# The recurrence's input copied out of PSUM by ScalarE before the scan, and V's bias folded into the output bias, in a transformer block fused with a mixture of experts

## The reference

```python
xn = _layernorm(x)
h = _layernorm(xn, ln1_g, ln1_b)
q, k, v = heads(h @ WQ + bQ), heads(h @ WK + bK), heads(h @ WV + bV)   # 16 heads of 8
scores = where(0 <= i - j < 128, q @ k.T / sqrt(8), -inf)
ao = softmax(scores) @ v
attn_out = ao @ WO + bO
u = h @ Bw                                    # 64 states
s_t = A * s_{t-1} + u_t                       # a scan over the 512 tokens
g = sigmoid(h @ Wg + bg)
x1 = xn + g * attn_out + (1 - g) * (s @ Cw)
s = x1 + gelu(_layernorm(x1, ln2_g, ln2_b) @ W1 + b1) @ W2 + b2
out = x + s * silu(mixture of 8 experts, top 2, of xn)
```

## Time and profile before

| | us |
|---|---|
| median of 3 runs (915.14 to 916.11) | 915.94 |
| the profiled execution, as timed | 917.65 |
| the same, its span in the trace | 915.9 |
| TensorE busy | 841.9 (92%) |
| VectorE busy | 712.3 (78%) |
| ScalarE busy | 721.0 (79%) |
| GpSimd busy | 484.2 (53%) |

### The profile page before, as it was taken

The page is one execution under the profiler, slowest core; times in us unless marked ns, Lnnn a source line. Parts: engine busy times, 40 slices in busy tenths (PEclk is TensorE's granted clock), DMA queues, the critical chain, the costliest instruction groups (busy, mean ns, idle before and its releaser), DMA issues.

```text
span 915.9 us, 37757 instructions
## 1 busy us (share of the span) xinstructions
PE 841.9 (92%) x15768; PEld 547.1 (60%) x15768; DVE 712.3 (78%) x1785; ACT 721.0 (79%) x1251; POOL 484.2 (53%) x786
## 2 busy tenths in 40 slices
PE   4569999999999999999999999999999999998996
PEld 2335666657566665756666575666657566665645
DVE  7666868879787887978788797878879787786635
ACT  4337888888788888888788888888888888877785
POOL 6417446382735638283653827366382736445352
PEclk9758999999999999999999999999999999999999
DMA  5952417133351613334261323416133341610101
GB/s 127 227 88 84 75 43 142 56 104 44 119 80 56 142 55 103 44 125 75 66 130 56 104 43 123 76 61 136 55 100 47 113 76 50 135 44 7 31 2 36
DMA packets 85597, 75.14 MB, mean 82 GB/s; under 512 B 9457, under 2 KB 79154, under 8 KB 85426
## 3 DMA queue, kind: packets, MB, share of 16 engines
q1 hardware_dynamic: 83346, 71.93, 34.9%
q10 hardware_dynamic: 2080, 0.79, 0.4%
HBM read 36.26 MB, written 30.15 MB: 73 GB/s over the span
## 4 chain that ended last, share of the span: by engine, by line
PE 64%; DVE 14%; issue 10%; ACT 7%; POOL 2%; DMA 2%; SPq 1%; POOLq 0%; DVEq 0%; ACTq 0%
PE ps L571 11%; PE ps L513 8%; PE ps L843 6%; PE ps L805 6%; PE ps L502 5%; PE ps L794 3%; PE ps L590 2%; DVE mx L1221 2%; PE ps L528 2%; PE ps L811 2%; PE ps L585 2%; ACT h L1077 2%; PE ps L719 2%; PE ps L781 2%; DVE act_t L1368 2%
## 5 line engine op out<-in xcount | busy, mean ns | idle before, releaser
L1221 DVE TENSOR_REDUCE mx<-ps 128x2 f32<-128x320 f32 (+1 forms) x512 | 219.7, 466 | 101.9 <-PE ps L528 100.8
L1004 ACT ACTIVATE pt<-ps 128x1024 f32<-128x1024 f32 (+1 forms) x256 | 232.9, 914 | 39.5 <-PE ps L502 37.2
L1487 POOL TENSOR_SCALAR_AFFINE_SELECT pt<-pt 128x512 f32<-128x512 f32 x256 | 162.3, 637 | 140.5 <-ACT pt L1004 139.5
L513 PE MATMUL ps<-kd,qz 48*32 48x160 bf16 (+1 forms) x4096 | 146.1, 236 | 13.8 <-issue 6.7
L502 PE MATMUL ps<-qz,kd 51*32 51x256 bf16 (+1 forms) x4096 | 153.6, 261 | 0.8 <-issue 0.7
L794 PEld LDWEIGHTS ps<-m,act_t 128*128 128x128 f32 x1024 | 128.1, 191 | 39.6 <-DVE act_t L1368 23.6
L571 PE MATMUL ps<-pt,va 128*32 128x256 f32 (+1 forms) x2048 | 145.2, 364 | 2.1 <-POOL pt L1490 0.9
L794 PE MATMUL ps<-m,act_t 128*128 128x128 f32 x1024 | 140.0, 280 | 7.6 <-DVE act_t L1368 5.7
L513 PEld LDWEIGHTS ps<-kd,qz 48*32 48x32 bf16 x4096 | 77.9, 92 | 105.9 <-issue 52.3
L1490 POOL TENSOR_SCALAR_AFFINE_SELECT pt<-pt 128x512 f32<-128x512 f32 x192 | 122.1, 636 | 0.0
L1037 ACT ACTIVATE lin<-ps,mbias 128x512 f32<-128x512 f32 x128 | 87.5, 684 | 35.5 <-DVE act_t L1368 22.9
(11 more groups left out here) (187 smaller groups left out, 1560.1 us busy)
## 6 DMA issues: line engine op xcount, KB each, us to landing
qz<-qk_parts SPq DMA_DIRECT2D x32, 384.0 KB, 6.4
kd<-qk_parts SPq DMA_DIRECT2D x32, 384.0 KB, 10.0
qk_parts<-qp SPq DMA_DIRECT2D x16, 384.0 KB, 3.1
qk_parts<-kp SPq DMA_DIRECT2D x16, 384.0 KB, 2.8
xl<-L_attn_x SPq DMA_DIRECT2D x16, 256.0 KB, 3.5
qk_parts<-qp SPq DMA_DIRECT2D x16, 256.0 KB, 3.1
qk_parts<-kp SPq DMA_DIRECT2D x16, 256.0 KB, 2.9
xnr<-xn SPq DMA_DIRECT2D x16, 256.0 KB, 2.5
```

The lines of the kernel that those rows point to most:

```text
L513: nc.tensor.matmul(ps[QG * c:QG * (c + 1), 4 + par, w * pr:w * (pr + 1)], qz[q][rows, 2 * g + pr, P * i + QG * c:P * i + QG * (c + 1)], kd ...
L1004: nc.scalar.activation(to, src, ACT.Exp, scale=SCALE).then_inc(exp_ok.sem, 1)
L1221: nc.vector.tensor_reduce(mx[:, i, HG * g + pr:HG * (g + 1):2], src, AX.X, ALU.max).then_inc(mx_ok.sem, 1)
L1487: sel1 = nc.gpsimd.affine_select(out=pt[:, s, :, 0:P], in_=pt[:, s, :, 0:P], compare_op=ALU.is_ge, fill=0.0, base=0, pattern=[[0, HG], [1, ...
```

## The change

Two things are changed.

**The scan's input.** From batch 2 on, ScalarE copies `u` (64 x 512 f32) from bank 7 into `h0` in SBUF (`u_out`, behind the exponential of chunk 8); `h0` is free there, since its rows were turned at chunk 3. `project_v` now waits for this copy (`u_in`) and no more for the scan. The scan reads `h0` and stands one chunk later in VectorE's order, behind the maxima of chunk 10 where it stood behind those of chunk 9. The last part of `route_mix` moves one chunk later too (`MIX`).

**V's bias.** `project_v` drops its bias matmul. At the start, one matmul of `bvc` (zero but for column 64, which is `bV`) with `WO` gives `bV @ WO` in row 64 of a bank, and `bias_out` adds it to the row of `ncw` that holds `bO`. What prepared `bV`'s bf16 parts is gone; the broadcast load of `bV` becomes a load of one column among the later weights.

```diff
-MIX = (9, 9, 13, 21)
+MIX = (9, 9, 13, 23)
...
             def project_v(m):
                 k = bank_of(m, "v")
-                pe.wait_ge(*(done(st_ok, m) if m >= 2 else done(v_ok, m - 1)))
+                pe.wait_ge(*(done(u_in, m - 2) if m >= 2 else done(v_ok, m - 1)))
...
-                add_bias(k, 0)
-                for t in range(NT):
-                    mm = nc.tensor.matmul(bank_t(k)[:, t], turned(m)[:, P * t:P * (t + 1)], wv[:], start=False, stop=True, skip_group_check=True)
+                for t in range(NT):
+                    mm = nc.tensor.matmul(bank_t(k)[:, t], turned(m)[:, P * t:P * (t + 1)], wv[:], start=True, stop=True)
...
                         logits(0)
+                        pe.wait_ge(*done(gth_ok, 1))
+                        nc.tensor.matmul(bank(7)[:, 0:P], bvc[:], wo[:], start=True, stop=True).then_inc(bvo_ps.sem, 1)
...
+            def u_out(m):
+                act.wait_ge(*done(u_ps, m))
+                act.wait_ge(*done(hT_ps, m))
+                act.wait_ge(*done(st_ok, m - 1))
+                nc.scalar.activation(h0[0:N].rearrange("p t d -> p (t d)"), bank(bank_of(m, "u"))[0:N], ACT.Copy).then_inc(u_in.sem, 1)
...
+                        if n == AT_U:
+                            u_out(b + 2)
...
-                for dst, src in ((wv, ob[:, 0]), (rows["bV"], ob[:, 1])):
-                    nc.vector.tensor_copy(dst[:].rearrange("p (s c k v) -> p s c k v", s=NS, c=HG, k=2), paired(src)).then_inc(values_set.sem, 1)
+                nc.vector.tensor_copy(wv[:].rearrange("p (s c k v) -> p s c k v", s=NS, c=HG, k=2), paired(ob[:, 0])).then_inc(values_set.sem, 1)
...
+            def bias_out():
+                dve.wait_ge(bvo_ps.sem, 1)
+                nc.vector.tensor_tensor(ncw[N:N + 1, :], ncw[N:N + 1, :], bank(7)[N:N + 1, 0:P], ALU.add).then_inc(bvo_ok.sem, 1)
...
             def recur(m):
 
-                dve.wait_ge(*done(u_ps, m))
+                if m < 2:
+                    dve.wait_ge(*done(u_ps, m))
+                    u = bank(bank_of(m, "u"))[0:N]
+                else:
+                    dve.wait_ge(*done(u_in, m - 2))
+                    u = h0[0:N].rearrange("p t d -> p (t d)")
                 dve.wait_ge(*done(ncw_ps, m - 3))
-                nc.vector.tensor_tensor_scan(st[0:N, (m) % 3], acol[0:N, :].to_broadcast([N, T]), bank(bank_of(m, "u"))[0:N], 0.0, ALU.mult, ALU.add).then_inc(st_ok.sem, 1)
+                nc.vector.tensor_tensor_scan(st[0:N, (m) % 3], acol[0:N, :].to_broadcast([N, T]), u, 0.0, ALU.mult, ALU.add).then_inc(st_ok.sem, 1)
...
-                            if step == 2 * AT_U + 3:
+                            if step == 2 * AT_V + 1:
                                 recur(b + 2)
```

More of the change, by code:

```diff
@@ L129, in build @@
         acol = sb("acol", [P, 1])
-        rows = {n: sb("row_" + n, [P, P]) for n in ("bV", "bg", "b2")}
+        rows = {n: sb("row_" + n, [P, P]) for n in ("bg", "b2")}
+        bvc = sb("bvc", [P, P])
         gbias_b = sb("gbias_b", [P, E], BF16)
@@ L221, in build @@
         values_set = signal("values_set", 1)
+        bvo_ps = signal("bvo_ps", 1)
+        bvo_ok = signal("bvo_ok", 1)
         ident_set = signal("ident_set", 1)
@@ L255, in build @@
         u_ps = signal("u_ps", 1)
+        u_in = signal("u_in", 1)
         g_ps = signal("g_ps", 1)
@@ L355, in build @@
             *((cols[n][:], col_of(a[n])) for n in ("ln1_g", "ln1_b", "bQ", "bK")), (acol[0:N, :], col_of(a["A"])),
-            (ob[:, 1], row_of(a["bV"])), (rows["bg"][:], row_of(a["bg"])), (cols["nw"][:], col_of(a["norm_weight"])),
+            (rows["bg"][:], row_of(a["bg"])), (cols["nw"][:], col_of(a["norm_weight"])),
         ]
@@ L361, in build @@
             (ncw[N:N + 1, :], a["bO"].rearrange("(o d) -> o d", o=1)),
+            (bvc[:, N:N + 1], col_of(a["bV"])),
             *((b2st[E * c:E * (c + 1), :], a["mlp2_bias"]) for c in range(NPART)),
@@ L372, in build @@
             (half[:], -0.5), (ident[:], 0.0), (identb[:], 0.0), (bw[:, N:], 0.0), (cw[N:, :], 0.0), (ncw[:], 0.0), (b2st[:], 0.0),
-            (edge[:], 0.0), (first[:], 0.0), (tie[:], 0.0), (sel[:], 0.0), (bias3[:], 0.0), (onesb[:], 1.0),
+            (edge[:], 0.0), (first[:], 0.0), (tie[:], 0.0), (sel[:], 0.0), (bias3[:], 0.0), (onesb[:], 1.0), (bvc[:], 0.0),
         ]
@@ L629, in project_g @@
                 pe.wait_ge(*done(ao_ok, m - 2, 1))
+                if m == 0:
+                    pe.wait_ge(bias_set.sem, 7)
                 add_bias(k, 1)
@@ L1180, in bias_setup @@
                 dve.wait_ge(blank_set.sem, len(BLANKS))
[L1181 to L1187, removed]
-                nc.vector.tensor_copy(nfn[:, 0:2 * P].rearrange("p (n d) -> p n d", n=2), ob[:, 2:4]).then_inc(bias_set.sem, 1)
+                nc.vector.tensor_copy(nfn[:, P:2 * P], rows["bg"][:]).then_inc(bias_set.sem, 1)
+                dve.wait_ge(bias_set.sem, 1)
+                nc.vector.tensor_tensor(ob[:, 3], rows["bg"][:], nfn[:, P:2 * P], ALU.subtract).then_inc(bias_set.sem, 1)
+                nc.vector.tensor_copy(bias3[0:1, 1], nfn[0:1, P:2 * P]).then_inc(bias_set.sem, 1)
+                dve.wait_ge(bias_set.sem, 3)
+                nc.vector.tensor_copy(nfn[:, P:2 * P], ob[:, 3]).then_inc(bias_set.sem, 1)
+                dve.wait_ge(bias_set.sem, 4)
+                nc.vector.tensor_copy(bias3[32:33, 1], nfn[32:33, P:2 * P]).then_inc(bias_set.sem, 1)
+                nc.vector.tensor_tensor(ob[:, 3], ob[:, 3], nfn[:, P:2 * P], ALU.subtract).then_inc(bias_set.sem, 1)
                 dve.wait_ge(bias_set.sem, 6)
-                nc.vector.tensor_copy(bias3[32:33], nfn[32:33, 0:2 * P].rearrange("p (n d) -> p n d", n=2)).then_inc(bias_set.sem, 1)
-                nc.vector.tensor_tensor(ob[:, 2:4], ob[:, 2:4], nfn[:, 0:2 * P].rearrange("p (n d) -> p n d", n=2), ALU.subtract).then_inc(bias_set.sem, 1)
-                dve.wait_ge(bias_set.sem, 8)
-                nc.vector.tensor_copy(bias3[64:65], ob[64:65, 2:4]).then_inc(bias_set.sem, 1)
+                nc.vector.tensor_copy(bias3[64:65, 1], ob[64:65, 3]).then_inc(bias_set.sem, 1)
+            def bias_out():
+                dve.wait_ge(bvo_ps.sem, 1)
+                nc.vector.tensor_tensor(ncw[N:N + 1, :], ncw[N:N + 1, :], bank(7)[N:N + 1, 0:P], ALU.add).then_inc(bvo_ok.sem, 1)
             def logits_in(m):
@@ L1268, in prologue @@
                 minus_maxima(0)
+                bias_out()
                 dve.wait_ge(masks_set.sem, N_MASKS)
```

8 lines of the change are left out of this document (5 added, 3 removed).

## The result

The changed kernel took 922.77 us (median of 4 runs, 921.46 to 924.32), the kernel before 915.92 in the same job: a ratio of 1.0065, 95% interval 1.0047 to 1.0082. It is slower. The profiled execution has a span of 922.6 us, against 915.9. That these spans lie so near the medians is chance: in every run the span is some 1.7 to 1.8 us shorter than the time, and both profiled executions were slower than their medians by nearly as much (917.65 against 915.94, 924.32 against 922.77). The difference of the spans, 6.7, is still that of the medians, 6.9, within 0.2.

A forecast was written before the change was run, and what follows sets the result against it. TensorE's wait for the scan was taken as the first bound, GpSimd's queue of selects as the second right behind it. 915.9 + 6.4 (loop, GpSimd held) - 1.1 (start) = 921.2 us; range 912.6 to 927.2.

The forecast's parts named there:

- What bounds the kernel: In each pass, TensorE's bias matmul waits for the scan (0.35 us in pass 6); GpSimd's queue is next.
- GpSimd's backlog: GpSimd's queue up to chunk 9's selects; the last ends 0.06 to 0.08 us ahead of `values(9)` in eight passes.
- Spared on TensorE: V's projection: 0.35 us of wait plus 0.19 of bias matmul, 0.54 a pass; without the hold, 1.4 us kept in all.
- ScalarE and the freed bank: Copy of `u` from PSUM, 0.60 us in ScalarE's idle time before chunk 9's exponential, ending before TensorE needs the bank: no cost.
- rival without a second bound: GpSimd's selects of chunk 9 come earlier with TensorE, all passes keep 0.54 us: 907.2 us; chance 0.04.
- The hold: The scan, with two SBUF inputs, holds k's split on GpSimd, delaying it and chunk 9's last select by 0.56 us.
- The sum: Later `values(9)` in the loop: 8 passes by 0.56 us, 4 by 0.47, none where 0.6 of room was: 6.4 us.
- the rival in which the scan comes too late: Scan waits for k's split, then holds the next GpSimd operation: some 0.9 us more in eight passes, 925.9 us; chance 0.08.
- The start: Prologue: without VectorE's copy `row_bV`, `norms(1)` begins 1.4 us earlier, less 0.3 for the `bvc` matmul: -1.1 us.
- The total: Whole kernel: 915.9 + 6.4 - 1.1 = 921.2 us; chance 0.57.
- The lock for a whole instruction: Skill's rule: VectorE and GpSimd share SBUF ports, locked per instruction; two SBUF inputs take part, a single one does not.

The follow-up runs named there:

- the late scan: Changed kernel with the scan moved behind the four operations on the maxima (after chunk 15), still with two SBUF inputs: 0.9987, 914.7 us.
- the exchange on GpSimd: Kernel before with k's split put ahead of `roots` on GpSimd, so that it falls into the scan reading `u` from PSUM: 0.9992, no difference.
- the kernel with both moves: Changed kernel with the scan behind the maxima's four operations and k's split behind the selects of chunk 15: 1.0100, 925.1 us.

## Why the prediction was right

**What bounds the kernel.** Right. The scan was the first bound (k's split moved alone in the kernel before gives nothing), GpSimd's backlog the second (moved alone in the changed kernel it gives 0.9% of the time). That the second was right behind, within 0.08 us in eight of the 14 passes, was the row on which the forecast turned.

**Spared on TensorE.** 0.54 us a pass ahead of `values(8)`: it starts at +14.74 us of the pass before and at +14.19 after, in the passes in which nothing else was late. None of it passes `values(9)`. The wait there was put at 1.1 us and is 0.89 in pass 6; another 0.12 stands ahead of the turn of the attention's output, for ScalarE, which the prediction did not have.

**ScalarE and the freed bank.** No cost was forecast, and the late scan shows none, with both in place and the loss gone. The copy was priced at 0.60 us and takes 0.59. Behind GpSimd, however, ScalarE's eviction of V is the third bound, which the prediction did not look for: its rival without a second bound, 907.2, could not have come true in full.

**The hold.** The scan was put at 406.0 to 407.13 of pass 6's old times; it came at 406.05 to 407.26 (408.88 - 2.83). The hold was put at 0.56 us and measured 0.63: the scan ends 0.13 later than I had it (0.05 of it the start, 0.08 the length, since I took its 1.13 us on the chain for 1.21), and GpSimd reads 0.19 and not 0.14 behind its start. That it holds at all was an extension from `dl`, a subtraction, to a scan; the exchange on GpSimd shows that the second SBUF input is what does it.

**The sum.** 6.4 us were forecast for the loop and 7.4 measured in the heads. The hold's size does not explain the missing 1.0: in passes in which nothing else was late (4, 6 and 10) the head grew by 0.57, as forecast, since of the 0.63 some 0.04 came back in the subtraction behind the split (1.20 us before, 1.16 after) and 0.02 in the gap ahead of `values(9)` (0.07 before, 0.05 after). By passes, pass 2 is 0.7 above its forecast, pass 7 is 0.4 and pass 11 is 0.5, and the other eleven together are 0.5 below theirs. Pass 11 had 0.75 us of room before, but after the change GpSimd came to k's split 0.6 later in that pass, for a reason not traced, and the room was gone. The two passes without the hold on the split, 2 and 7, are the rival in which the scan comes too late, each by another turn. TensorE was late in both, and with it the maxima and the scan:

```profile
194.25 1.16 POOL L1472 TENSOR_TENSOR kp<-kr,kp 128x512 bf16<-128x512 f32 x1
195.36 1.56 POOL L1512 TENSOR_SCALAR_AFFINE_SELECT pt<-pt 128x512 f32<-128x512 f32 x1
...
194.50 1.98 DVE L1236 TENSOR_TENSOR_SCAN st<-acol,h 64x512 f32<-64x512 f32 x1
...
463.76 2.10 POOL L1472 TENSOR_TENSOR kp<-kr,kp 128x512 bf16<-128x512 f32 x1
...
463.70 1.21 DVE L1236 TENSOR_TENSOR_SCAN st<-acol,h 64x512 f32<-64x512 f32 x1
```

In pass 2 GpSimd's subtraction was first by 0.25 us; the scan waited for its end and then held the select behind it (1.56 instead of 0.64): that head grew by 1.21 us. In pass 7 the scan was first by 0.06 and held the subtraction (2.10 instead of 1.16): that head grew by 0.38, from the 0.68 us of room there. The rival was sized rightly, as a thing of single passes and not of the whole loop. That the holds alone make these two heads is read from the rows; the other passes scatter by some tenths that I did not trace. So the loop's figure, near as it is, rests in part on luck: errors of 1.6 one way and 0.5 the other. The +0.4 behind the 14 passes, too, was not forecast and has not been traced.

**The start.** -1.1 forecast, -1.12 measured; the copy is shown to be the cause, but the agreement to 0.02 is luck. It hangs on 0.1 us of order in the prologue, and in the executions without the long copy the first `values(0)` lies anywhere from 71.77 to 73.37, which is later than the 73.05 of before.

**The total.** 921.2 was forecast on the scale of the span and 922.6 measured there; the 1.4 us are the loop's 1.0 and the 0.4 at the end.

## What to carry to other kernels

Before a wait is removed, ask what ends next behind it and by how much: 0.54 us spared on TensorE a pass were worth next to nothing, since another queue ended 0.07 us later. An operand that moves from PSUM to SBUF can turn a VectorE operation into one that stops GpSimd, or is stopped by it; look at what begins inside it on the other engine, and move either of the two to where the other's queue has room, not to where the first engine is merely idle. Of two bounds that stand close, taking either away alone gives little: here the change alone cost 0.65%, the later split alone gave nothing, and both together gave 0.26%.

## What the runs showed of the hardware

The hold goes both ways, and between wide operations the order of start decides it, though not to the hundredth: GpSimd's subtraction of 1.16 us, begun 0.15 us ahead of the scan, stretched it to 2.18, and the scan, begun 0.06 us ahead, stretched that subtraction to 2.10; but GpSimd's addition `ob`, begun only 0.05 us ahead of `dl` by the record, is the one that lost time there (0.33 us), and `dl` lost none.

An operation of GpSimd on 4 columns is held as a wide one is (0.19 to 1.07 us), but it is not shown to hold. In pass 6 of the changed kernel the last step of `roots`, 1.02 us long, began 0.73 us ahead of the scan and ran for 0.29 us beside it (408.15 and 408.88 in the rows above), and the scan took its 1.21; so it was in 12 of the 14 passes. VectorE's product `act_t`, with two SBUF inputs, took its usual 0.69 us in all 16 passes of the kernel before in which it began inside such a step:

```profile
427.25 1.01 POOL L1433 TENSOR_TENSOR r<-r3t,half 128x4 f32<-128x4 f32 x1
...
427.50 0.69 DVE L1368 TENSOR_TENSOR act_t<-lin,gc 128x512 f32<-128x512 f32 x1
```

The lock for a whole instruction, by which the prediction words the rule, does not show in these rows; why is not tested.

The second input need not be large: `acol` is one column of 64 values, read again for each of the 512 steps, and counts as an SBUF input. Single-input operations are in it as well: VectorE's copy from SBUF to SBUF beside GpSimd's memset is one, and the cast of `nm` another, beside k's split (0.65 us at 418.52 in the kernel with both moves, 0.22 at 414.20 with the scan late alone):

```profile
418.52 0.65 DVE L1254 CAST nm<-mr 128x64 bf16<-128x64 f32 x1
...
414.20 0.22 DVE L1254 CAST nm<-mr 128x64 bf16<-128x64 f32 x1
```

The same section of the Trainium skill ("SBUF — State Buffer", "Who interferes with whom") counts copies and casts among the operations that can take the shared ports; these rows agree, and they are what the prediction's short wording of the rule (a single SBUF input takes no part) left out.
